# Turning softmax row shifts on VectorE instead of TensorE, half-array filler products, and a list scheduler with other array-form costs, in a one-core macaron transformer layer

## The reference

```python
x = x + 0.5 * ffn(layernorm(x))
x = x + attn(layernorm(x))
x = x + 0.5 * ffn(layernorm(x))
# ffn: silu((x @ gate_w.T) * gate_s) * ((x @ up_w.T) * up_s) @ down_w.T * down_s, INTER = 704
# attn: q, k, v = x @ W.T; rotary embedding on q and k; causal
#       softmax(q k^T / 4) v per head; @ Wo.T
```

## Time and profile before

| | us |
|---|---|
| median of 3 runs | 888.81 (888.66 to 890.97) |
| profiled execution, its own time | 890.0 |
| span of its trace | 888.2 |
| TensorE busy | 845.6 (95%) |
| VectorE busy | 643.0 (72%) |
| ScalarE busy | 557.7 (63%) |
| GpSimd busy | 376.8 (42%) |
| mean granted clock | 0.984 of full speed |

### The profile page before, as it was taken

One profiled execution on the slowest core, in us unless ns is written; L12 is line 12 of the kernel. 1 busy time (PEld: TensorE's weight loads), 2 busy tenths in 40 slices (PEclk: granted clock), 3 DMA queues, 4 the chain that ended last, 5 costly groups with the idle time before them and its releaser, 6 DMA issues.

```text
span 888.2 us, 17639 instructions
## 1 busy us (share of the span) xinstructions
PE 845.6 (95%) x6426; PEld 565.2 (64%) x6426; DVE 643.0 (72%) x1273; ACT 557.7 (63%) x1096; POOL 376.8 (42%) x355
## 2 busy tenths in 40 slices
PE   7999999999999999999989999999999999999996
PEld 6788888775654555555545566454554546888885
DVE  5767678876989988688889878788878902655442
ACT  4765645355567767556847565777567876665652
POOL 1758685453243434151243441321231324656553
PEclk9999999998999999899979999999999999999999
DMA  9701233008265165352443716432641111001001
GB/s 320 287 1 72 84 95 107 4 13 218 75 181 172 49 171 146 121 163 76 91 127 131 195 37 159 111 97 67 199 111 40 39 52 32 29 24 44 30 24 50
DMA packets 61956, 89.80 MB, mean 101 GB/s; under 512 B 14892, under 2 KB 27564, under 8 KB 61612
## 3 DMA queue, kind: packets, MB, share of 16 engines
q1 hardware_dynamic: 61724, 88.57, 33.9%
q10 hardware_dynamic: 144, 0.07, 0.0%
HBM read 45.52 MB, written 40.76 MB: 97 GB/s over the span
## 4 chain that ended last, share of the span: by engine, by line
PE 77%; DVE 12%; ACT 5%; issue 3%; DMA 1%; POOL 1%; SPq 1%; DVEq 0%; POOLq 0%; ACTq 0%
PE psum L860 14%; PE psum L971 13%; PE psum L923 11%; PE psum L954 10%; PE psum L830 10%; PE psum L886 9%; PE psum L839 5%; DVE NP L1203 5%; PE psum L933 2%; DVE ST L1111 2%; ACT XN L1012 2%; PE psum L846 2%; ACT PT L1083 2%; DVE HF_f L1154 1%; DMA X<-x 1%
## 5 line engine op out<-in xcount | busy, mean ns | idle before, releaser
L1203 DVE TENSOR_REDUCE NP<-psum 128x1 f32<-128x512 f32 (+3 forms) x640 | 363.6, 627 | 68.8 <-PE psum L933 50.6
L1083 ACT ACTIVATE PT<-psum 128x512 f32<-128x512 f32 (+2 forms) x640 | 307.9, 568 | 155.2 <-PE psum L954 153.5
L1299 POOL TENSOR_SCALAR_AFFINE_SELECT PT<-PT 128x512 f32<-128x512 f32 x128 | 80.7, 638 | 229.8 <-ACT PT L1083 176.7
L954 PE MATMUL psum<-Q,K 50*128 50x512 f32 (+2 forms) x768 | 142.3, 411 | 7.3 <-ACT PT L1083 4.5
L860 PE MATMUL psum<-XH,WG_f 128*128 128x512 f32 x352 | 142.6, 405 | 5.9 <-DVE HF_f L1154 5.1
L923 PE MATMUL psum<-K,Q 48*128 48x512 f32 (+2 forms) x768 | 144.5, 406 | 3.6 <-DVE NP L1203 1.3
L971 PE MATMUL psum<-PT,V 128*32 128x512 f32 (+3 forms) x1536 | 146.2, 499 | 0.7 <-ACT PT L1083 0.5
L860 PE MATMUL psum<-XL,WG_f 128*128 128x512 f32 x352 | 138.5, 393 | 0.0
L1256 POOL TENSOR_TENSOR HL_f<-HF_f,HH_f 128x512 fp32r<-128x512 f32 x80 | 102.9, 1296 | 79.8 <-ACT HH_f L1041 79.8
L1154 DVE SCALAR_TENSOR_TENSOR HF_f<-psum,US,G_f 128x512 f32<-128x512 f32 x96 | 71.2, 750 | 64.7 <-PE psum L860 29.0
L923 PEld LDWEIGHTS psum<-K,Q 48*128 48x128 f32 x768 | 69.8, 187 | 64.9 <-DVE NP L1203 25.1
(11 more groups left out here) (77 smaller groups left out, 1081.2 us busy)
## 6 DMA issues: line engine op xcount, KB each, us to landing
zd<-ZH SPq DMA_DIRECT2D x32, 512.0 KB, 4.6
Q<-zd SPq DMA_DIRECT2D x64, 192.0 KB, 3.8
K<-zd SPq DMA_DIRECT2D x64, 192.0 KB, 4.9
zd<-ZL SPq DMA_DIRECT2D x16, 512.0 KB, 5.1
od<-OS SPq DMA_DIRECT2D x32, 256.0 KB, 2.6
OC<-od SPq DMA_DIRECT2D x32, 128.0 KB
SC<-rd_ SPq DMA_DIRECT2D x32, 128.0 KB
out<-X SPq DMA_DIRECT2D x16, 256.0 KB, 2.1
```

What stands on the lines that cost most here:

```text
L954: ins = tn.matmul(dst, K[k][r, p, j * P:(j + 1) * P], Q[k][r, p, 512 * c2 + base:512 * c2 + 512], start=True, stop=True)
L1083: sc.activation(dst, src, ACT.Exp, scale=0.25).then_inc(S["act_exp"], 1)
L1203: ve.tensor_reduce(out=acc, in_=src, axis=AX, op=ALU.max, negate=True).then_inc(S["dve_max"], 1)
L1299: gp_.affine_select(out=pt, in_=pt, compare_op=ALU.is_ge, fill=0.0, base=0, pattern=[[0, 4], [1, P]], channel_multiplier=-1).then_inc(S["p ...
```

## The change

The change has three parts.

1. **Row shifts.** `pe_nT` and `act_nt` are gone, with their PSUM bank and their semaphores. `dve_nm` gets one more instruction, a VectorE transpose in 32x32 blocks from NM (128x32) to NMT, now 128x32. It waits for the low part just made (`dve_nl`) and for the landing of the previous group's `dma_nw`. `dma_nw` waits for `dve_nm` and writes NMT in 128 rows of 128 bytes instead of 32 rows of 512 bytes; what lies in DRAM is the same. The wait of `dve_nm` for `pe_nT` two groups back is gone.
2. **Fillers.** A filler behind a half, masked or col product is planned as "half" and uses 64 rows (contraction of 64) instead of 128; behind a full product it is as before. It goes by choice to an open bank that a filler already used, and real products are given such banks first.
3. **The scheduler.** Other simulated costs: changes of form between half and full now cost 170 and 175 ns (190 and 30 before), score products with a mask have a form of their own ("mask") with its change costs, TensorE restarting after an idle moment costs 90 ns, the per-column price of score products falls from 0.443 to 0.4167 ns, `pe_pv` gets 94 ns more, and the busy shares by which fillers are counted differ. MODE_PLACE is unchanged, and half and mask count as the same form when a piece is chosen. The emitted order therefore differs.

```diff
@@ Timetable.settle
+            some = (lone + [b for b in open_ if b not in lone])[:want[0]]
+            return tuple(sorted(some, key=lambda b: b not in filled))
...
-                cost = item[0] + (0 if self.mode[item[2]] == mode[0] else MODE_PLACE) - URGE.get(kind, (0,) * 9)[held.get(kind, 0)]
+                cost = item[0] + MODE_PLACE * MODE_COST.get((ARRAY[mode[0]], ARRAY[self.mode[item[2]]]), 0) - URGE.get(kind, (0,) * 9)[held.get(kind, 0)]
...
-            b = open_[-1]
+            b = next((b for b in open_ if b in filled), open_[-1])
+            filled.add(b)
-            self.ns[piece], self.mode[piece], self.room[piece], self.empties[piece] = (430 if now < WARM_COLD else 220), mode[0], None, ()
+            self.ns[piece], self.mode[piece], self.room[piece], self.empties[piece] = (430 if now < WARM_COLD else 220), FILL[mode[0]], None, ()
...
-                        if self.mode[piece] != mode[0]:
-                            ns += MODE_NS[mode[0], self.mode[piece]]
-                            mode[0] = self.mode[piece]
+                        change = MODE_NS.get((mode[0], self.mode[piece]), 0)
+                        ns += max(change, RELOAD_NS * (free[e] < now))
+                        mode[0] = self.mode[piece]
...
-MODE_NS = {("full", "half"): 190, ("col", "half"): 110, ("half", "full"): 30, ("half", "col"): 30, ("full", "col"): 60, ("col", "full"): 60}
+MODE_NS = {("full", "half"): 170, ("col", "half"): 105, ("half", "full"): 175, ("half", "col"): 117, ("full", "col"): 70, ("col", "full"): 70,
+           ("half", "mask"): 23, ("mask", "half"): 82, ("full", "mask"): 186, ("col", "mask"): 126, ("mask", "full"): 214, ("mask", "col"): 145,
+           ("mask", "mask"): 103}
+RELOAD_NS = 90
-BUSY = {"full": 0.92, "half": 0.8, "col": 1.0}
+BUSY = {"full": 0.92, "half": 0.85, "mask": 0.75, "col": 0.95}
+FILL = {"full": "full", "half": "half", "mask": "half", "col": "half"}
...
@@ maxima
-            add(key, 350 + 150 * c2, "dve_nm", gr, c2, after=drained + ([("pe_nT", gr - 2, c2)] if gr >= 2 else []))
-            add(key, 120, "pe_nT", gr, c2, after=[("dve_nm", gr, c2)], room=(1,))
-            add(key, act_ns(P) + 20, "act_nt", gr, c2, after=[("pe_nT", gr, c2)] + ([turn_of("nw", *was)] if gr else []), empties=[("pe_nT", gr, c2)])
+            add(key, 450 + 150 * c2, "dve_nm", gr, c2, after=drained + ([turn_of("nw", *was)] if gr else []))
...
@@ tensor_program, pe_warm
-                    tn.matmul(bank(*piece)[:, 0:P], IDT[:, :], IDT[:, :], start=True, stop=True)
+                    r = slice(0, P if plan.mode[piece] == "full" else 64)
+                    tn.matmul(bank(*piece)[:, 0:P], IDT[r, :], IDT[r, :], start=True, stop=True)
...
@@ vector_program, dve_nm
-                    ve.tensor_tensor(shift_parts(gr, c2, 1), src, f32(shift_parts(gr, c2, 0)), ALU.subtract).then_inc(S["dve_nm"], 1)
+                    ve.tensor_tensor(shift_parts(gr, c2, 1), src, f32(shift_parts(gr, c2, 0)), ALU.subtract).then_inc(S["dve_nl"], 1)
+                    e.wait_ge("dve_nl", *a)
+                    if gr:
+                        e.wait_ge(*turn_of("nw", gr - 1, c2))
+                    both = f32(NM[gr % 2][:, c2, :, :, :, :]).rearrange("p a b c t -> p (a b c t)")
+                    ve.transpose(NMT[c2][:, :], both).then_inc(S["dve_nm"], 1)
...
@@ sync_program, nw
-                    e.wait_ge("act_nt", *a)
+                    e.wait_ge("dve_nm", *a)
-                    sy.dma_start(NMD[c2], f32(NMT[c2][:, :])).then_inc(sem, 16)
+                    sy.dma_start(NMD[c2].rearrange("r (k n) -> k r n", k=4), NMT[c2][:, :]).then_inc(sem, 16)
```

More of the change, by code:

```diff
@@ L226, in ready_later @@
             return any(x not in self.began for x in by_place[-1:])
-        warmed = set()
+        warmed, filled = set(), set()
         while todo or ends:
@@ L248, in settle @@
                             warms += 1
-                            free[e] = now + self.ns[piece]
-                            spent.append((now, free[e]))
+                            ns = self.ns[piece] + max(MODE_NS.get((mode[0], self.mode[piece]), 0), RELOAD_NS * (free[e] < now))
+                            mode[0] = self.mode[piece]
+                            spent.append((now, now + self.ns[piece]))
+                            free[e] = now + ns
                             self.order[e].append(piece)
@@ L265, in settle @@
                                 holders[b] = piece
+                                filled.discard(b)
                             if self.room[piece] == (2,):
@@ L284, in settle @@
             later = [free[e] for e in self.order if free[e] > now and (ready[e] or e == "PE" and todo)] + [x[0] for x in ends]
-            if todo and free["PE"] <= now:
+            if todo and ends and free["PE"] <= now:
                 later.append(now + 100)
@@ L294 @@
 MODE_PLACE, WAIT_NS, DMA_RATE, WINDOW = 1.14, 80, 200.0, 56.5
[L295 removed]
+MODE_NS = {("full", "half"): 170, ("col", "half"): 105, ("half", "full"): 175, ("half", "col"): 117, ("full", "col"): 70, ("col", "full"): 70,
+           ("half", "mask"): 23, ("mask", "half"): 82, ("full", "mask"): 186, ("col", "mask"): 126, ("mask", "full"): 214, ("mask", "col"): 145,
+           ("mask", "mask"): 103}
+RELOAD_NS = 90
+MODE_COST = {("full", "half"): 1, ("col", "half"): 1, ("half", "full"): 1, ("half", "col"): 1, ("full", "col"): 1, ("col", "full"): 1}
 AHEAD = 4.3
 WARM_SPAN, WARM_SHARE, WARM_COLD = 2700.0, 0.59, 10000.0
[L298 removed]
+BUSY = {"full": 0.92, "half": 0.85, "mask": 0.75, "col": 0.95}
+FILL = {"full": "full", "half": "half", "mask": "half", "col": "half"}
+ARRAY = {"full": "full", "half": "half", "mask": "half", "col": "col"}
 URGE = {"pe_s": (12, 12, 12, 12, 4, 0, 0), "pe_st": (12, 12, 8, 8, 0, 0, 0)}
@@ L491, in maxima @@
                 done += n
[L492 to L495, removed]
+                sets = 2 if u == "a" else 1
+                add(key, sets * (max(s_width(t, ch), 256) * 0.4167 + (26 if ch < c2 else 80)), "pe_s", *unit, after=[ld(gr, ch), ld(gr, c2), ("act_mk",)],
+                    room=(2,), mode="half" if ch < c2 else "mask")
                 for hh in range(2):
@@ L535, in heads @@
                 else:
-                    w = sum({0: 865, 128: 652, 256: 438, 384: 250}[e_skip(c2, i)] for i in (j - 1, j))
+                    w = 94 + sum({0: 865, 128: 652, 256: 438, 384: 250}[e_skip(c2, i)] for i in (j - 1, j))
                     first = j == 1
@@ L661, in macaron @@
         NM = [place(f"NM{i}", [P, 2, 2, 2, 2, 4], F32R) for i in range(2)]
-        NMT = [place(f"NMT{i}", [32, P], F32R) for i in range(2)]
+        NMT = [place(f"NMT{i}", [P, 32]) for i in range(2)]
         SU, RC = ([place(f"{n}{i}", [P, 16]) for i in range(2)] for n in ("SU", "RC"))
@@ L934, in tensor_program @@
                     ins.then_inc(S["pe_s"], 1)
-                elif kind == "pe_nT":
-                    gr, c2 = a
-                    e.wait_ge("dve_nm", gr, c2)
-                    take(piece)
-                    src = f32(NM[gr % 2][:, c2, :, :, :, :]).rearrange("p a b c t -> p (a b c t)")
-                    tn.transpose(bank(*piece)[0:32, 0:P], src, IDT[:, :]).then_inc(S["pe_nT"], 1)
                 elif kind == "pe_st":
@@ L1063, in scalar_program @@
                     sc.activation(dst, bank("pe_v", b, cc, 2 * pr).rearrange("p (j h n) -> p j h n", j=2, n=HD), ACT.Copy).then_inc(S["act_v"], 1)
-                elif kind == "act_nt":
-                    gr, c2 = a
-                    e.wait_ge("pe_nT", *a)
-                    if gr:
-                        e.wait_ge(*turn_of("nw", gr - 1, c2))
-                    sc.activation(NMT[c2][:, :], bank("pe_nT", *a)[0:32, 0:P], ACT.Copy).then_inc(S["act_nt"], 1)
                 elif kind == "act_exp":
```

11 lines of the change are left out of this document (4 added, 7 removed).

## The result

The kernel after takes 901.63 us, the median of 10 runs (894.74 to 910.28), beside 889.39 us for the kernel before (10 runs, 885.20 to 892.87): a ratio of 1.013, interval 1.010 to 1.015. It is 1.3% slower. The forecast was 871 us, 2% faster, so both sign and range (860 to 890) were wrong.

A forecast was written before the change was run, and what follows sets the result against it. TensorE, busy 95%, was taken as the bound, paced with VectorE. Terms 16.6 + 15 - 2.5 = 29.1 us, 60% kept: 890.0 - 17.5 = 872.5, less 1.2 for the median, so 871 us; range 860 to 890.

The forecast's parts named there:

- The new order: Whole kernel: changed scheduler costs and swapped pieces were priced at zero, with up to 12 us either way.
- The bound: For the order's worth: three half-clock stretches, 23.9 us in all; losing them gains up to 12 us, three more cost that.
- Fillers in the half form: Attention, 190 to 756 us: 92 filler blocks save 0.30 us each, 27.6 at most; 60% taken, 16.6 us.
- a sign of trouble: Fillers in the whole kernel: the prediction called itself wrong if their number rises much; no size given.
- The transpose on TensorE: Line 940 removed from TensorE: 11.2 us of stream plus 3.8 of its waiting, 15 us saved.
- Rival B: Attention: time freed from fillers and transpose becomes waits for reductions; a small gain, 884 us; chance 0.14.
- The transpose on VectorE: 32 new VectorE transposes of 0.24 us, 7.7 us, ahead of the next reductions; a third counted, 2.5 us lost.
- The port rule: VectorE with one SBUF input outside two-port modes shares no port pair with GpSimd, so transposes cost 7.7 us, not 12.1.
- The copy on ScalarE and the shift DMA: Removed copy frees 8.3 us of ScalarE, nothing on the path; DMA in 128 rows of 128 bytes, no gain or loss.
- Rival D: Attention, above all 700 to 756: 64-row fillers hold the clock less well; slower, 895 us with seven more half-clock stretches; chance 0.12.
- the bound of 0.97: Attention: the prediction called itself wrong if the granted clock falls below 0.97.
- The 60% for two engines that pace each other: Attention: TensorE and VectorE would wait for each other more, so 60% of the 29.1 us sum was taken, 17.5 us.

The follow-up runs named there:

- c: Kernel before, its order kept, with both edits: half-form fillers and transposes on VectorE instead of TensorE; 881.9 us, ratio 0.991.
- a: Kernel before, its order kept, with half-form fillers only, transposes still on TensorE; 876.6 us, ratio 0.985.
- o: Kernel a replanned with the scheduler's WAIT_NS at 70 instead of 80, a meaningless change giving another order; 881.0 us, ratio 0.992.
- g: Kernel a replanned with the scheduler's WINDOW at 57.0 instead of 56.5, a meaningless change giving another order; 893.2 us, ratio 1.003.
- m: Kernel e replanned with the scheduler's AHEAD at 4.4 instead of 4.3, a meaningless change giving another order; 886.1 us, ratio 0.996.
- e: Kernel after, with new costs and half-form fillers, but shifts turned on TensorE and copied on ScalarE as before, and planned so; 915.0 us, ratio 1.030.
- r: Kernel c with ScalarE's high-part copy reading a constant tile without waiting, and the output projection using the low part three times; 876.7 us, ratio 0.985.
- q: Kernel after, own order, with ScalarE's high-part copy reading a constant tile without waiting, output projection using the low part three times; 890.2 us, ratio 1.000.
- j: Kernel after, its order kept, with each filler product made twice; 901.3 us, ratio 1.012.
- d: Kernel after, its order kept, with all fillers using 128 rows; 901.9 us, ratio 1.013.
- i: Kernel before, its order and full fillers kept, without the TensorE transpose and its copy; shifts go out unturned, no VectorE transpose; 890.1 us, ratio 0.999.
- k: Kernel before, its order kept, with fillers behind half and col products left out and those behind full ones kept; 879.6 us, ratio 0.987.

## Why the prediction was wrong

**The step that failed** is "The new order", priced at zero, with 12 us to either side by way of the clock. It measured 19.7 us (c to after). I had it that costs of the scheduler are no work of the chip, and that is true; but the order decides what waits at the head of each list, and this kernel has 1,122 pieces on TensorE, of which 525 stand elsewhere after the change. The bound took the clock for the only thing that an order can move. The clock did move, from 0.977 to 0.966 in the medians of c and after, which is some 8 us by the slope above, an estimate, and within the 12. The greater part is not clock, and for that the prediction had no term. The profile of before had the sign of it, if not the size: the earlier trace rows lists waits of TensorE and VectorE for each other, both ways, and an order decides which of them meet. Draws of one cost table spread over 17 us (a, o, g) or 29 (m, e), more than the 12 I allowed. Of all orders run with half-form fillers that of the kernel before was the fastest (a); nothing in the rows of the kernel before tells that.

The 19.7 us, as far as they are shown: 6.2 go with the wait of ScalarE for the late reciprocals (11.4 less 5.2), some of it by way of the clock. In the profiled executions c and after differ by 16.4 us of span: 1.9 ahead of the first exp, 10.9 in between, 3.6 after the last. r and q, without the wait, differ by 13.1: 1.2, 8.5 and 3.4. So some 5 us arise outside attention. Up to 190 us and from 756 us on every filler is full in both plans, and of the edits there are only two transposes of 0.21 us ahead of the first exp, which c has as well; what differs is the plan, in which 26 TensorE pieces ahead of the first key-by-query product and 56 behind the last stand elsewhere. The prediction had held that nothing changes there. The other 8.5 us in attention stay open. Longer waits for reductions are not the reason on their own: over all of TensorE's lines they are 67.1 us in after and 77.5 in c, though the longest at the query-by-key products have grown (2.2 us against 0.9). 51 us at half clock in eight stretches between 190 and 756 us, where c has 31 in five, go with it, but no run takes these away by themselves.

**Fillers in the half form, 16.6 us by 60%, 10 us.** Right: 12.8 us in the old order. The size of one saving was less than I had worked out: two records took 0.33 us where I had 0.22, though three in 0.31 agree with 0.11 a record, and 12.8 us over 92 blocks are 0.14 each where I had 0.30. Their number rose from 188 to 214 (two records each in both traces, 376 and 428), which I had named as a sign of trouble; j, with twice as many products, takes no longer. In the new order d and after are equal, and the clock shows why the gain does not appear: with the half form it is 0.013 lower.

**The transpose on TensorE, 15 us.** Wrong: i takes 0.7 us more than before, within the interval of no change, so the term measured nothing. Rival B's mechanism, freed time that becomes waits for reductions, is what happened here, and waits for ScalarE came with it. It stood in the text with 0.14.

**The transpose on VectorE, +2.5 us.** Right: +2.4 and +5.3. The instruction took 0.211 us, not 0.24, and never longer than 0.214, beside a neighbour of up to 2.25. The port rule cited above from the Trainium skill, "SBUF — State Buffer", agrees with that.

**The copy on ScalarE and the shift DMA, 0.** Not told apart from the rest: i has both, and shows no difference. The DMA's issue does cost more on SP, 549 ns in the median where the 32-row form took 335, and nothing in the chain shows it.

**Rival D, the clock.** The granted clock did fall, 0.95 in the stage, below the bound of 0.97 that I had named as a sign. Its mechanism, half-form fillers that hold the clock less well, shows in the new order (0.960 to 0.972 in the runs of after, 0.970 to 0.985 with full fillers in d) and not in the old one (a and before). By itself it does not make the change slower: d, with full fillers and the clock mostly back, takes 901.9 us, and j, with the clock all back, 901.3. It is what hides the fillers' gain. D stood in the text with 0.12, and as the text has it, by six or more further stretches at half clock; there were five.

**The 60% for two engines that pace each other** was the right thought, applied to the sum and not to its parts: it is about 77% for the fillers and 0 for the transposes. The two edits together, in the old order, gave 7.5 us (c), not 17.5. So even at a price of zero for the order the forecast of 871 us was 11 us too low, though 882 lies within its range.

The fastest kernel run is a, 876.6 us: the half-form fillers alone, in the old order.

## What to carry to other kernels

When an edit comes with a new schedule, first run the edit in the frozen old order, and the schedule with a meaningless constant moved: here such a constant was worth up to 29 us, the edits 13. In fixed in-order lists look for cheap pieces that wait for something slow at the head of an engine's list (here a copy of 0.63 us that held up ScalarE for 5.7); their place costs more than their work. And an engine busy 95% gives back freed time only where the pieces behind it are ready: read who the freed instruction's successor waits for before counting it. Compare the clock over all runs of a kernel, not in one profiled execution: d's profiled one, with 0.970, is the lowest of its six, and taken alone it hides that full fillers held the clock better.

## What was not expected of the hardware

The block transpose of 128x32 floats took 211 to 214 ns in all 32 cases, with neighbours of up to 2.25 us. Issuing a DMA of 128 rows of 128 bytes took 0.55 us on SP against 0.34 for 32 rows of 512. Between kernels the granted clock said little on the time: those whose profiled executions had 0.972 (k, 879.6 us) and 0.984 (a, 876.6 us) are faster than those with 0.982 (i, 890.1 us) and 0.985 (j, 901.3 us). Between runs of one kernel it said most: 0.68 us for each 0.001.
